# Layer 2 of a four-layer graph network: another place for the values product, other engine orders, and another order of the stacking transfers

## The reference

```python
qkv = h @ W                                   # h (16, 512, 128), W (128, 384)
q, k, v = qkv.reshape(Bn, Nn, 3, H, HEAD_DIM).transpose(2, 0, 3, 1, 4)
mask = jnp.where(adj == 0, -jnp.inf, 0.0)
scores = jnp.einsum('bhid,bhjd->bhij', q, k) / np.sqrt(HEAD_DIM) + mask
attn = jax.nn.softmax(scores, axis=-1)
out = jnp.einsum('bhij,bhjd->bhid', attn, v)
x = _layernorm(x + out, axis=-1)
```

## Time and profile before

| | us |
|---|---|
| median of 3 runs (lowest, highest) | 998.18 (997.38, 1002.39) |
| the profiled execution's own time | 995.78 |
| span of its trace | 994.0 |
| PE busy in the span | 899.7 |
| DVE, ACT, POOL busy | 645.7, 501.5, 387.6 |

### The profile page before, as it was taken

How to read it: one execution, slowest core, us unless ns; L and a number is a source line. 1 busy time by engine, 2 the same in 40 slices (tenths; PEclk the granted TensorE clock), 3 DMA queues, 4 the chain that set the end, 5 groups by cost and what they waited for, 6 DMA issues and landing times. The chain is left out here.

```text
span 994.0 us, 20920 instructions
## 1 busy us (share of the span) xinstructions
PE 899.7 (91%) x6020; PEld 638.7 (64%) x6036; DVE 645.7 (65%) x2014; ACT 501.5 (50%) x902; POOL 387.6 (39%) x439
## 2 busy tenths in 40 slices
PE   6999999999999799794589999999999987899994
PEld 5799999999998778542344454445544434667663
DVE  4755554554555766563657777777777636888985
ACT  4322121212213155482357777777777656767762
POOL 4011021021110030001166787787877672545455
PEclk9999999999999799996679999999999999999998
DMA  8000000000000100000134243333324320010111
GB/s 238 22 12 12 22 12 13 21 11 11 21 0 11 33 0 0 1 0 1 32 75 88 64 89 70 80 79 75 85 64 92 69 64 2 22 32 21 32 32 32
DMA packets 34217, 40.63 MB, mean 41 GB/s; under 512 B 6656, under 2 KB 17536, under 8 KB 34176
## 3 DMA queue, kind: packets, MB, share of 16 engines
q1 hardware_dynamic: 33072, 40.00, 16.8%
q10 hardware_dynamic: 1104, 0.13, 0.1%
HBM read 6.43 MB, written 4.19 MB: 11 GB/s over the span
## 5 line engine op out<-in xcount | busy, mean ns | idle before, releaser
L1667 DVE CUSTOM_DVE_ANT_0 junk<-bank,mask_ij 128x512 bf16<-128x512 f32 x256 | 166.7, 688 | 82.7 <-PE bank L1749 81.1
L1533 POOL TENSOR_TENSOR half_sum<-prob 128x1024 f32<-128x1024 f32 x64 | 151.8, 2380 | 11.6 <-ACT prob L1605 11.6
L1605 ACT ACTIVATE prob<-wide 128x1024 f32<-128x1024 f32 x128 | 125.2, 1017 | 37.9 <-PE wide L1766 34.6
L430 ACT CAST yT<-wide 128x512 fp32r<-128x512 f32 x48 | 28.1, 588 | 206.1 <-PE wide L824 156.8
L529 POOL TENSOR_TENSOR Xr<-Xf,Xr 128x512 fp32r<-128x512 f32 x16 | 20.4, 1290 | 168.2 <-ACT Xr L425 167.9
L1749 PE MATMUL bank<-qkT 32*128 32x512 f32 x256 | 66.9, 518 | 20.5 <-DVE mx L1667 17.8
L152 POOL TENSOR_SCALAR n_rstd<-n_aggr 128x4 f32<-128x4 f32 x32 | 6.7, 209 | 188.1 <-DVE n_aggr L145 177.8
L1762 PE MATMUL wide<-qk_st 128*128 128x512 f32 x256 | 76.9, 422 | 0.7 <-ACT prob L1605 0.3
L1362 PEld LDWEIGHTS bank<-Wh,pr 128*128 128x128 f32 x512 | 59.5, 191 | 25.6 <-issue 21.8
L1362 PE MATMUL bank<-Wh,pr 128*128 128x129 f32 x512 | 63.7, 278 | 13.1 <-ACT pr L1246 13.1
L58 PE MATMUL bank<-z,L3T_hi 128*128 128x256 f32 x256 | 73.7, 288 | 0.1
(11 more groups left out here) (281 smaller groups left out, 2280.9 us busy)
## 6 DMA issues: line engine op xcount, KB each, us to landing
qk_st<-qkT SPq DMA_DIRECT2D x192, 128.0 KB, 2.4
out_dram<-rc SPq DMA_DIRECT2D x16, 256.0 KB, 2.3
Xf<-X SPq DMA_DIRECT2D x14, 256.0 KB, 2.3
A<-in_adj_dram SPq DMA_DIRECT2D x4, 256.0 KB, 5.0
qk_st<-neg_row SPq DMA_DIRECT2D x64, 2.0 KB
Xf<-in_x_dram SPq DMA_DIRECT2D x2, 256.0 KB, 6.9
mask_q<-mask_ji SPq DMA_DIRECT2D x16, 32.0 KB, 1.8
w<-in_L_gnn_W_dram SPq DMA_DIRECT2D x2, 128.0 KB, 2.3
```

The source lines that it names most:

```text
L1533: pool.tensor_tensor(flat(half_sum[h][:]), flat(prob[bp][h][:, 0:2]), flat(prob[bp][h][:, 2:4]), ALU.add).then_inc(h_sum, 1)
L1605: act.activation(flat(prob[bp][h][:, 2 * half:2 * half + 2]), wide[half][:], ACT.Exp, scale=SCALE).then_inc(t_exp, 1)
L1667: dve.tensor_tensor_reduce(out=junk[hh][:], in0=bank[4 + hh][:], in1=m.mask_ij[:, i], scale=1.0, scalar=3.0 * MASKED, op0=ALU.add, op1=ALU ...
```

## The change

Six edits. (1) PE's list begins with V0 and spreads V0 to V3 between s0 and s1; m and D come after them, D behind s2; t0 moves from the head of the list to its end with one step less back, which is the same place in the stream. (2) SP's list: the three transfers of head 1 come ahead of those of head 0, those of heads 3 and 2 follow at once, and the two rows of heads 3 and 2 come last. (3) ACT takes `xT` out first and makes `xT_hi` from that SBUF copy; kh stands ahead of vc, y ahead of E0. (4) DVE computes kl behind u0, B ahead of u7 and b behind u1. (5) POOL's list begins with g1 and r, S0 stands ahead of xl, S1 to S3 come last. (6) The buffer r has two copies, so that c2 waits for the y of two batches before; to make place, some small tensors of layers 2 and 3 lie elsewhere. The written-out end is rearranged to match.

```diff
-        PE_ORDER = staged("t0:3 s0:2 m:3 D0:4 D1:4 V0:4 V1:4 s1:2 t1:3 s2:2 V2:4 V3:4 s3:2 x:1 t2:3 s4:2 n:2 d:4 o:4 "
-                          "s5:2 T:0 q:1 t3:3 s6:2 k:1 v:2 s7:2")
+        PE_ORDER = staged("V0:4 s0:2 V1:4 V2:4 s1:2 V3:4 m:3 t1:3 s2:2 D0:4 D1:4 s3:2 x:1 t2:3 s4:2 n:2 d:4 o:4 "
+                          "s5:2 T:0 q:1 t3:3 s6:2 k:1 v:2 s7:2 t0:2")
-        SP_ORDER = staged("st3:1 dn1:0 st0:0 dn0:0 st1:0 dn3:0 dn2:0 st2:0")
+        SP_ORDER = staged("dn2:1 dn1:0 st1:0 dn0:0 st0:0 st3:0 st2:0 dn3:0")
...
-                    pool.wait_ge(x_c, after(b, 1))
+                    pool.wait_ge(x_hi, after(b, 1))
...
-            tail("r.14 S2.15 S3.15 g2.14", POOL_ORDER, work, None)
+            tail("r.14 g2.14", POOL_ORDER, work, None)
...
-                    act.wait_ge(x_ps, after(b, 1))
+                    act.wait_ge(x_c, after(b, 1))
                     act.wait_ge(k_ps, after(b - 1, 1))
-                    act.copy(xTr[0][:], ring["x"][:]).then_inc(x_hi, 1)
+                    act.copy(xTr[0][:], xT[bp][:]).then_inc(x_hi, 1)
...
-                    dve.wait_ge(norm.s_x, after(b - 1, 4))
-                    dve.tensor_tensor(r[:].rearrange("p t (h d) -> p t h d", h=H),
+                    dve.wait_ge(norm.s_x, after(b - 2, 4))
+                    dve.tensor_tensor(r[bp][:].rearrange("p t (h d) -> p t h d", h=H),
...
-            tail("3x0.0 V0.15 V1.15 V2.15 V3.15 3w0.0 3w1.0 3j0.0 3i0.0 o.15 D0.15 D1.15 3x0.1 d.15 3w0.1 3w1.1 3e0.0 3e1.0 "
-                 "3j0.1 3i0.1 3e2.0 3e3.0", PE_ORDER, work, item)
+            tail("V0.15 V1.15 V2.15 V3.15 3x0.0 D0.15 D1.15 3w0.0 3w1.0 d.15 o.15 3j0.0 3i0.0 3x0.1 3e0.0 3e1.0 "
+                 "3w0.1 3w1.1 3e2.0 3e3.0 3j0.1 3i0.1", PE_ORDER, work, item)
```

More of the change, by code:

```diff
@@ L1116, in layer3 @@
     rl = [over("rl0", [P, NT, N]), nc.alloc_sbuf_tensor_at("rl1", [P, NT, N], F32, offset=rl1_at)]
+    s12 = [over(f"s12{k}", [P, NT, 2]) for k in range(2)]
+    s2s = [over(f"s2s{k}", [P, 2, NT]) for k in range(2)]
+    mx = [over(f"mx3{k}", [P, NT]) for k in range(2)]
+    em = [over(f"em{k}", [P, 3, NT]) for k in range(2)]
+    rec = [over(f"rec3{k}", [P, NT]) for k in range(2)]
     at[0] = 205120
     pr = [over(f"pr{k}", [P, NT, N]) for k in range(2)]
[L1119 to L1123, removed]
     norm = Norm(nc, own, m, "n3")
@@ L1401, in layers2_3 @@
         v = [sb(f"v{k}", [P, NT, D]) for k in range(2)]
-        junk = [sb(f"junk{k}", [P, N], BF16) for k in range(2)]
-        mx = [sb(f"mx{k}", [P, TILES]) for k in range(2)]
+        junk = [nc.alloc_sbuf_tensor_at("junk0", [P, N], BF16, offset=221952), sb("junk1", [P, N], BF16)]
+        mx = [nc.alloc_sbuf_tensor_at(f"mx{k}", [P, TILES], F32, offset=221504 + k * TILES * 4) for k in range(2)]
         neg_row = [sb(f"neg_row{k}", [2 * NT, P], F32R) for k in range(2)]
@@ L1412, in layers2_3 @@
         rec = sb("rec", [P, NT, H, 1])
-        r = sb("rb", [P, NT, D])
+        r = [sb(f"rb{k}", [P, NT, D]) for k in range(2)]
         on = sb("on", [P, N])
@@ L1438, in layers2_3 @@
         block = own.enter_context(nc.Block())
-        PE_ORDER = staged("t0:3 s0:2 m:3 D0:4 D1:4 V0:4 V1:4 s1:2 t1:3 s2:2 V2:4 V3:4 s3:2 x:1 t2:3 s4:2 n:2 d:4 o:4 "
-                          "s5:2 T:0 q:1 t3:3 s6:2 k:1 v:2 s7:2")
-        ACT_ORDER = staged("kh:2 E0:3 mr:3 N:0 E1:3 Y:1 e:4 E2:3 E3:3 y:5 f:4 xh:1 xc:1 nr:2 E4:3 E5:3 qh:1 E6:3 E7:3 vc:2")
-        DVE_ORDER = staged("u5:2 R:0 ql:1 u6:2 u7:2 kl:1 B:0 u0:1 b:4 u1:1 u2:1 u3:1 u4:1 c1:3 c2:3")
-        POOL_ORDER = staged("xl:1 r:4 S2:3 X:1 S3:3 g1:0 g2:4 S0:2 S1:2")
-        SP_ORDER = staged("st3:1 dn1:0 st0:0 dn0:0 st1:0 dn3:0 dn2:0 st2:0")
+        PE_ORDER = staged("V0:4 s0:2 V1:4 V2:4 s1:2 V3:4 m:3 t1:3 s2:2 D0:4 D1:4 s3:2 x:1 t2:3 s4:2 n:2 d:4 o:4 "
+                          "s5:2 T:0 q:1 t3:3 s6:2 k:1 v:2 s7:2 t0:2")
+        ACT_ORDER = staged("f:4 E2:3 E3:3 N:0 e:4 xc:1 xh:1 nr:2 E4:3 E5:3 qh:1 E6:3 E7:3 kh:1 vc:2 y:5 E0:2 E1:2 Y:0 mr:2")
+        DVE_ORDER = staged("b:5 u2:2 u3:2 u4:2 c1:4 c2:4 u5:2 R:0 ql:1 u6:2 B:0 u7:2 u0:1 kl:1 u1:1")
+        POOL_ORDER = staged("g1:0 r:4 X:1 S0:2 xl:0 g2:4 S1:2 S2:2 S3:2")
+        SP_ORDER = staged("dn2:1 dn1:0 st1:0 dn0:0 st0:0 st3:0 st2:0 dn3:0")
         RING = [(name, back) for name, back in PE_ORDER if name in ("T", "x", "q", "k", "v", "n", "m", "D0", "V0", "d", "o")]
@@ L1538, in work @@
                     hold(pool, gate)
-                    pool.tensor_tensor(flat(r[:]), flat(r[:]), batch_flat(m.X, b), ALU.add).then_inc(o_r, 1)
+                    pool.tensor_tensor(flat(r[bp][:]), flat(r[bp][:]), batch_flat(m.X, b), ALU.add).then_inc(o_r, 1)
             run(pool, POOL_ORDER, work, last=17)
@@ L1573, in work @@
                 elif name == "y":
-                    norm.apply_act(act, b + CREDIT, bp, r, lambda k: tile_of(m.X, b, k))
+                    norm.apply_act(act, b + CREDIT, bp, r[bp], lambda k: tile_of(m.X, b, k))
                 elif name == "xh":
-                    act.wait_ge(x_ps, after(b, 1))
+                    act.wait_ge(x_c, after(b, 1))
                     act.wait_ge(k_ps, after(b - 1, 1))
-                    act.copy(xTr[0][:], ring["x"][:]).then_inc(x_hi, 1)
+                    act.copy(xTr[0][:], xT[bp][:]).then_inc(x_hi, 1)
                 elif name == "xc":
@@ L1624, in _ @@
             item = third.act_items(act)
-            tail("3x0.0 f.15 3w0.0 3w1.0 y.14 3l0.0 3l1.0 e.15 3l2.0 3l3.0 3g0.0 3x0.1 3w0.1 3w1.1 3E0.0 3E1.0 "
-                 "3l0.1 3l1.1 3l2.1 3l3.1 3g0.1 y.15", ACT_ORDER, work, item)
-            pairs(act, B, 3, third.in_order(item), first=2)
+            tail("f.15 3x0.0 e.15 3w0.0 3w1.0 y.14 3l0.0 3l1.0 3l2.0 3l3.0 3g0.0 y.15", ACT_ORDER, work, item)
+            pairs(act, B, 3, third.in_order(item), first=1)
         @block.vector
@@ L1684, in work @@
                     dve.wait_ge(o_r, after(b, 1))
-                    norm.statistics(dve, b + CREDIT, bp, r)
+                    norm.statistics(dve, b + CREDIT, bp, r[bp])
                     norm.aggregate(dve, b + CREDIT, bp)
-            run(dve, DVE_ORDER, work, last=17)
+            run(dve, DVE_ORDER, work, last=18)
             third.dve_credits(dve)
             item = third.dve_items(dve)
-            tail("b.14 3w0.0 3w1.0 3m0.0 3m1.0 3m2.0 3m3.0 3c0.0 3c1.0 3c2.0 c1.15 c2.15 3e0.0 3e1.0 3w0.1 3w1.1 b.15 "
-                 "3e2.0 3e3.0 3m0.1 3m1.1 3m2.1 3m3.1 3c0.1 3c1.1 3c2.1", DVE_ORDER, work, item)
-            pairs(dve, B, 3, third.in_order(item), first=2)
+            tail("b.14 3w0.0 3w1.0 c1.15 c2.15 3m0.0 3m1.0 3m2.0 b.15 3m3.0 3c0.0 3c1.0 3c2.0", DVE_ORDER, work, item)
+            pairs(dve, B, 3, third.in_order(item), first=1)
         @block.tensor
```

## The result

| | before | after |
|---|---|---|
| median (lowest, highest), 4 runs each | 998.04 (997.38, 1002.39) | 1028.53 (1027.41, 1031.28) |
| the profiled execution's own time | 995.78 | 1027.41 |
| span of its trace | 994.0 | 1025.6 |

The changed kernel takes 1.0294 times as long, 95% interval [1.026, 1.0327]: slower, as forecast, but by some 30 us where 12.6 were forecast, and outside the range of 996 to 1021.

A forecast was written before the change was run, and what follows sets the result against it. PE's list was taken as the clock of layer 2's even part. 14 steps of +0.68 (9.5), batch 15's step 1.8 and the end 1.3 gave +12.6 us: 1008.4 on the profiled 995.78, median 1010.5, range 1003.5 to 1018, with rivals 996 to 1021.

The forecast's parts named there:

- The new SP order: Layer 2's even steps: t0 waits 1.18 us for its transfers, starting 8.62 us behind n instead of 7.44.
- (a): Rival, chance 0.13: a smaller wait at t0 (0.7) and the gain of spacing cancel; about 998 us.
- (b): Rival, chance 0.10: no wait for the transfers at t0, so the savings are all gain; 987 us.
- The new PE order: Between t0 and the next n: 0.5 us of waits saved from 13.02, bounds 0 and 0.8.
- PE's clock: Rival, chance 0.01: a fifth of the steps at 1.2 GHz, PE's part growing by some 50 us.
- What was called hidden: Moved copies, DVE items, POOL sums and mr fit into idle time or slack; mr priced 0, upper bound 0.3 us.
- rival (c): Chance 0.10: the loop from D1 through POOL's sums to t2 doesn't close in a step; 1 us more each, 1025.
- Batch 15's step: Step without T, q or k: n to t0 8.62 us instead of 6.34, 0.5 saved, so +1.8.
- The end of the layer: Passage to layer 3: its copies follow POOL's four half sums, costing 1.3 us, bounds -1 and 4.
- The sum: Whole kernel: 9.5 + 1.8 + 1.3 = 12.6 us slower.

The follow-up runs named there:

- e1: Changed kernel with the transfers of heads 0 and 1 exchanged back in SP's list, all else as changed: 1001.79 us, ratio 0.9994 to the kernel before.
- e5: Kernel before with only the blocks of heads 0 and 1 exchanged in SP's list: 1022.12 us, ratio 1.0192.
- e8: Kernel before with head 0's row and transfers ahead of head 1's row in SP's list: ratio 0.9984.
- e4: Changed kernel with five unused mask products on PE ahead of t0's wait for its transfers: 1024.40 us, ratio 1.0209 to the kernel before.
- e2: Changed kernel with POOL's three memsets of layer 3's constants ahead of the last batch's half sums: 1022.39 us, ratio 1.0198 to the kernel before.
- after_again: Changed kernel run a second time, unchanged, on another chip: 1029.20 us, ratio 1.0276 to the kernel before.

## Why the prediction was wrong in size

**The new SP order: right.** The wait was forecast as 8.62 us from n to t0. From batch 6 to batch 13 the changed kernel has 8.63 to 8.78, and e1 and e5 show that this one exchange makes it and unmakes it. Up to batch 5 it is 8.92 to 9.38: there the transfers land later (a median of 2.8 us for the last two of head 0 in batch 4, where the forecast took 2.4), for a reason that stays open. The mean of 8.80 is 0.18 more than forecast. Counting the landing from the start of the issue, with the reader 0.09 behind, was good to 0.02 us in the step shown. Rivals (a) and (b), which needed a smaller wait or none, are out.

The Trainium skill, "DMA: Bandwidth & Descriptors", section "Rules for kernel authors" (issue early, wait late) pointed the same way, and the runs agree where a reader waits: in e8, where none does, issuing earlier still gave nothing.

**The new PE order: mis-sized.** From 13.02 I took off 0.5 for waits that would go; e1 measures 12.86 against 12.98, so it is 0.12. The waits did go. The step that failed is that I priced the moved products as if their length were the same in any place. PE of e1 in a step without the loop's jump:

```profile
614.34 1.20 PE L1760 MATMUL wide<-qk_st 128*128 128x512 f32 x4
...
615.84 1.06 PE L1782 MATMUL bank<-prob,v 128*32 128x512 f32 x8
616.84 0.50 PE L1747 MATMUL bank<-qkT 32*128 32x512 f32 x2
...
619.55 1.07 PE L1782 MATMUL bank<-prob,v 128*32 128x512 f32 x8
620.55 0.27 PE L1752 MATMUL bank<-ident,mx 128*8 128x128 f32 x1
620.58 1.17 PE L1760 MATMUL wide<-qk_st 128*128 128x512 f32 x4
...
622.04 0.50 PE L1747 MATMUL bank<-qkT 32*128 32x512 f32 x2
622.47 1.92 PE L1772 MATMUL bank<-half_sum,ones_hd 128*32 128x512 f32 x16
624.33 0.50 PE L1747 MATMUL bank<-qkT 32*128 32x512 f32 x2
```

By starts, and against the step of before that begins at 616.96: t0 takes 1.50 instead of 1.65, m 0.03 instead of 0.24, t1 1.46 instead of 1.66. That is 0.56 saved, a little more than the 0.5 that I had counted on. But V0 and V3 now stand alone and take 1.00 each, V1 and V2 together 1.85, and the two D behind a pair s 1.86; in the kernel before, D took 1.74 and the two pairs of V 1.83 and 1.85. Together that is 5.71 instead of 5.42. So 0.29 goes back. The waits of the score pairs' weight loads for DVE were no guide: over 12 steps they grew from 27.0 us to 37.9 in e1, and the pairs from s0 to s4 still take 0.43 each.

The loop takes the rest. In every other step V0 is the first product behind the loop's jump and starts 0.25 to 0.30 us late, with "issue" as the releaser, as in the changed kernel at 650.29:

```profile
649.60 0.43 PE L1764 MATMUL wide<-mask_q,identb 32*32 32x512 bf16 x16
650.29 1.07 PE L1782 MATMUL bank<-prob,v 128*32 128x512 f32 x8 [0.25 <-issue]
```

In the changed kernel's nine steps at full clock, t0 to n takes 12.76 in the mean, 0.24 more than the forecast 12.52, and n to t0 8.79, 0.17 more. The clean step is therefore 21.55 instead of 21.14, +0.41 in each of 12.

**PE's clock: the rival that I gave 0.01.** I argued from the earlier trace rows that a stretch with PE busy for 40.33 of 50 us had a clock of 1.00, so steps with 19 of 21 busy would keep it. That mean says nothing of how the idle time lies: the changed kernel has one gap of 1 to 1.9 us ahead of each t0, and the clock fell behind three of twelve (of 1.40, 1.66 and 1.26 us), with PE busy for 89 to 94% of the 50 us around them. The Trainium skill, "TensorE: Matmul & The Clock Gate", section "What's actually happening", ties the clock to PE's recent activity; the trace agrees: in e4, with the gap filled, all 12 steps of the traced execution have 1.00. I also mis-priced the rival: a step in which the clock falls doesn't run at half speed throughout, only for a few us, and costs 1.4 to 2.3 more, not twice PE's part. It came to 5.3 us in the even steps, not 50.

**What was called hidden: right.** The loop of rival (c) closes. t2 shows no wait for a transfer, and POOL, which the loop runs through, has its idle time in one place, ahead of S0. Waits from 560 to 780 in the changed kernel (total, times, longest):

```profile
POOL half_sum L1533 <- PE bank L1772: 56.4, 10, 7.2
...
PE wide L1760 <- DMA qk_st<-qkT: 12.4, 10, 1.7
```

The second line's 10 waits are the t0 of the 10 steps, and no t of another head.

**Batch 15's step: right.** Forecast +1.8, measured 21.05 - 19.16 = +1.89, with 8.60 us from n to t0 where 8.62 was forecast.

**The end of the layer: a wait overlooked.** I forecast +1.3 with bounds -1 and 4, and it was +8.57. The change put the four half sums ahead of the copies for layer 3, and I priced only the copies. The memsets move with them, and PE's whole tail, V of batch 15 first, stands behind a wait for these. Of the 8.57, e2 gives back 4.8 by moving the memsets alone. The rest, some 3.8, goes with the clock: e2's 40.94 is what e5 takes with the old order at the same clock of 0.88, and only the execution profiled of before had 1.00 there. So none of it need be owed to the new order of the end, though PE now waits 4.79 us for layer 3's `dg`, where before it waited 2.78 for `pr` at the first L1362. That is read from one execution of each; no run was made for it.

**The sum.** Forecast 12.6, measured 31.6 in the span. The 19.0 between them: 7.3 the end of the layer (4.8 of its 8.57 the memsets), 2.9 the saving of the PE order that wasn't there and 2.0 later landings (together 0.41 in 12 steps), 5.3 the clock in these steps. These make 17.5; the fill and the rest of the span (1.69 and 1.04 us more than before, of which 14 minus 12 steps of 0.68 had been counted) account for the remaining 1.5, batch 15 included. Executions of one kernel differ by as much there. The steps of the prediction that failed are thus, the largest first: the clock priced at nothing (5.3 us, and by the comparison above some 3.8 more in the end), the memsets not followed to their reader (4.8), and the PE order's saving (2.9).

## What to carry to other kernels

When a DMA queue is reordered, list its blocks by the time of their first reader: t0's block as the last of four costs its wait in every step, and exchanging two blocks (e1) took the changed kernel from 2.9% slower to no difference. When work is moved on one engine, follow every semaphore set behind it, a constant's memset too, to the engine that waits for it, and ask what stands behind that wait. A gap of 1 to 2 us in PE costs its own length and sometimes as much again in clock, so look at how the gaps lie, and not at the busy share alone. When products are moved, the saved waits are only one side: read what the same products take alone and behind another neighbour.

## What the runs showed that was not expected

- The clock fell behind gaps of 1.25 to 2.31 us in a PE that was busy for 81 to 94% of the 50 us around them, but not behind each: 3 of 12 in the changed kernel, whose gap of 1.87 us left it whole, and the same gap of 2.31 us ahead of the same V gave 3.64 us (clock whole) in one execution and 5.34 in another. The shortest gaps, 1.00 to 1.04 us in every other step from batch 6 to 12 of after, after_again and e2, were never followed by a fall. What decides it was not found.
- Five products whose result nobody reads, 1.25 us of PE's idle time, made a kernel shorter by 5.4 us between the same marks, in one execution of each.
- The first product behind the loop's jump starts 0.25 to 0.30 us late, with nothing but "issue" as releaser, when it is one of V's. In the kernel before t0 stands in that place and starts 0.04 to 0.07 us late.
